# Attention with two sequences per tile: the weighted values of both in one full-width product per pair of heads

## What is computed

```python
attn = jax.nn.softmax(jnp.einsum('bhsd,bhtd->bhst', q, k) / sqrt(8), axis=-1)
out = jnp.einsum('bhst,bhtd->bhsd', attn, v)              # weighted values
out = out.transpose(0, 2, 1, 3).reshape(B, -1, D)
x = x + jnp.tanh(g_xattn) * (out @ Wo.T + bo)
```

## Time and profile before

| | before |
|---|---|
| median of 3 runs | 936.67 us (935.26 to 936.72) |
| the profiled execution's own time | 936.35 us |
| its span, first to last instruction | 934.5 us |
| busy share PE / DVE / ACT / POOL | 97% / 87% / 79% / 70% |
| TensorE's granted clock | 0.996 of full |

### The profile page before, as it was taken

The page is one execution under the profiler, slowest core; times in us unless marked ns, Lnnn a source line. Parts: engine busy times, 40 slices in busy tenths (PEclk is TensorE's granted clock), DMA queues, the critical chain, the costliest instruction groups (busy, mean ns, idle before and its releaser), DMA issues. The chain is left out here.

```text
span 934.5 us, 32489 instructions
## 1 busy us (share of the span) xinstructions
PE 906.0 (97%) x11654; PEld 736.1 (79%) x11654; DVE 811.1 (87%) x2348; ACT 742.8 (79%) x1617; POOL 652.9 (70%) x1184
## 2 busy tenths in 40 slices
PE   6999999999999999999899999999999999999996
PEld 3888788788889999998786777777777777777774
DVE  6898888899979998899778988898988868888886
ACT  5888888888887777776676788788878877888885
POOL 5787878776635566565989878778786638777773
PEclk9999999999999999999999999999999999999999
DMA  3501010100000000000000000000000003333333
GB/s 117 189 26 48 26 47 26 47 14 26 13 2 2 1 1 2 1 1 1 2 13 14 14 26 14 26 14 14 26 14 14 4 7 66 82 78 80 78 78 82
DMA packets 54270, 31.15 MB, mean 33 GB/s; under 512 B 38368, under 2 KB 46816, under 8 KB 54112
## 3 DMA queue, kind: packets, MB, share of 16 engines
q1 hardware_dynamic: 54112, 29.08, 11.7%
HBM read 16.48 MB, written 4.19 MB: 22 GB/s over the span
## 5 line engine op out<-in xcount | busy, mean ns | idle before, releaser
L1011 DVE TENSOR_REDUCE smax<-score 128x16 f32<-128x1024 f32 x128 | 156.6, 1224 | 44.7 <-PE score L1441 23.9
L1382 PEld LDWEIGHTS bank<-vb,prob_t 128*64 128x64 f32 x4096 | 130.2, 138 | 49.4 <-issue 40.9
L1023 DVE TENSOR_TENSOR prob<-score,smax 128x512 f32<-128x512 f32 x256 | 163.4, 680 | 0.4
L657 ACT ACTIVATE prob_t<-bank 128x512 f32<-128x512 f32 x256 | 139.1, 595 | 20.2 <-PE bank L1357 6.5
L652 ACT ACTIVATE prob<-prob 128x512 f32<-128x512 f32 x256 | 147.5, 632 | 5.4 <-DVE prob L1023 5.4
L1382 PE MATMUL bank<-vb,prob_t 128*64 128x18 f32 x4096 | 142.5, 212 | 0.1
L1357 PE MATMUL bank<-const,prob 128*128 128x128 f32 x1024 | 133.8, 274 | 0.7 <-DVE x_all L1124 0.7
L1357 PEld LDWEIGHTS bank<-const,prob 128*128 128x128 f32 x1024 | 116.4, 141 | 1.8 <-DVE x_all L1124 1.1
L736 ACT ACTIVATE eb_t<-eb,gwt 128x128 f32<-128x128 f32 x256 | 81.5, 390 | 40.0 <-POOL eb_acc L503 26.3
L663 ACT ACTIVATE o_t<-bank,b_col 128x128 f32<-128x128 f32 x128 | 48.8, 381 | 65.9 <-PE bank L1357 65.7
L435 POOL TENSOR_SCALAR kj<-k_sb,const 128x512 f32<-128x512 f32 x124 | 85.2, 694 | 20.7 <-issue 20.7
(11 more groups left out here) (171 smaller groups left out, 2335.3 us busy)
## 6 DMA issues: line engine op xcount, KB each, us to landing
ctx_t<-in_ctx SPq DMA_DIRECT2D x32, 256.0 KB, 2.7
x_all<-in_x SPq DMA_DIRECT2D x16, 256.0 KB, 3.4
out_x<-x_all SPq DMA_DIRECT2D x64, 64.0 KB, 1.8
ew<-in_ew SPq DMA_DIRECT2D x2, 512.0 KB, 6.0
q2t<-q2b SPq DMA_TRANSPOSE x64, 2.5
f_cw<-in_f_cw SPq DMA_DIRECT2D x1, 768.0 KB, 7.6
w_t<-in_w_attn SPq DMA_DIRECT2D x2, 256.0 KB, 4.2
f_w<-in_f_w SPq DMA_DIRECT2D x2, 256.0 KB, 7.0
```

Of the source, the lines that this page charges most:

```text
L657: act.activation(prob_t[:, 4 * half:4 * half + 4, :].rearrange("p i q -> p (i q)"), bank[(PT, PT2)[half]], ACT.Copy).then_inc(s["p_copied" ...
L1011: dve.tensor_reduce(smax[:].rearrange("p (r h) -> p r h", r=RH), sc, AX.X, ALU.max).then_inc(s["smax_done"], 1)
L1023: dve.tensor_tensor(prob[:, par, half * 512:(half + 1) * 512].rearrange("p (r h k) -> p r h k", r=2, k=S), sc[:, g], m.unsqueeze(3).to_bro ...
L1382: last = pe.matmul(bank[OV][q, i * 2 * VW:(i + 1) * 2 * VW], prob_t[:, i, q], vb[:, k // G, v0 + b * NPAIR + i, :, :].rearrange("p h v -> ...
```

## The change

The two products of a pair of heads become one. The stationary operand is all 128 columns of `prob_t` (both batches' queries), the streamed one the 18 columns of batch 0 and the 18 of batch 1, so the result is 128 x 2 x 18: each query row gets its weighted sum over the values of its own batch and one over those of the other batch, which is of no use. `divide` divides both (256 instead of 128 elements per partition); the denominator is the same for both. `transpose_o`, before a single transposition of 128 x 128, becomes two ordinary products with 64 columns of the identity each: the one for batch b has `o_n` of batch b as its stationary operand and streams the columns of the identity that pick the query rows of batch b.

The transposed outcome moves from the bank of the weighted values (`OV`) to the first columns of the bank `PT2`, which the second half of `transpose_p` also uses. `o_t` gets two buffers. In TensorE's program `transpose_o` now stands before `project_o`. Waits: the second half of `transpose_p(n)` now also waits for `o_copied` (`copy_o` of tile n-1); `transpose_o(n)` waits for `copy_o` of tile n-1 and for the copy of a second half from `PT2`; `values` no longer waits for `o_copied`; `divide` waits for `project_o` instead of `copy_o`.

```diff
-        o_tr_ps, wo_ps = bank[OV][:, 2 * P:3 * P], bank[OV][:, 3 * P:4 * P]
+        o_tr_ps, wo_ps = bank[PT2][:, 0:P], bank[OV][:, 3 * P:4 * P]
+        ov_ps = bank[OV][:, 0:BT * H * VW].rearrange("p (b c) -> p b c", b=BT)
...
-        o_n = sb("o_n", [P, 2, P])
-        o_t = sb("o_t", [P, P])
+        o_n = sb("o_n", [P, 2, BT, P])
+        o_t = sb("o_t", [P, 2, P])
...
             def divide(n, k):
-                ov = bank[OV][:, 0:H * VW].rearrange("p (h v) -> p h v", h=H)
+                ov = ov_ps.rearrange("p b (h v) -> p b h v", v=VW)
                 wait(dve, "pv_mm", n + 1)
-                wait(dve, "o_copied", n)
+                wait(dve, "wo_mm", n - 1)
...
-                dve.tensor_tensor(o_n[:, k % 2, :].rearrange("p (h v) -> p h v", h=H), ov[:, :, 0:HD],
-                                  rden[:].unsqueeze(2).to_broadcast([P, H, HD]), ALU.mult)\
+                dve.tensor_tensor(o_n[:, k % 2].rearrange("p b (h v) -> p b h v", v=HD), ov[:, :, :, 0:HD],
+                                  rden[:].unsqueeze(1).unsqueeze(3).to_broadcast([P, BT, H, HD]), ALU.mult)\
...
             def transpose_p(n, k, half):
                 wait(pe, "exp_done", 2 * n + half + 1)
                 wait(pe, "p_copied", 2 * n + half - 1)
+                if half:
+                    wait(pe, "o_copied", n - 1)
...
-                wait(pe, "o_copied", n - 1)
                 for i in range(NPAIR):
...
-                    for b in range(BT):
-                        q = slice(b * S, (b + 1) * S)
-                        last = pe.matmul(bank[OV][q, i * 2 * VW:(i + 1) * 2 * VW], prob_t[:, i, q],
-                                         vb[:, k // G, v0 + b * NPAIR + i, :, :].rearrange("p h v -> p (h v)"),
-                                         start=True, stop=True, skip_group_check=True)
+                    last = pe.matmul(ov_ps[:, :, i * 2 * VW:(i + 1) * 2 * VW], prob_t[:, i, :],
+                                     vb[:, k // G, v0 + i:v0 + BT * NPAIR:NPAIR, :, :].rearrange("p b h v -> p b (h v)"),
+                                     start=True, stop=True, skip_group_check=True)
...
             def transpose_o(n, k):
                 wait(pe, "o_norm", n + 1)
-                tr(o_tr_ps, o_n[:, k % 2, :]).then_inc(s["o_tr"], 1)
+                wait(pe, "o_copied", n)
+                wait(pe, "p_copied", min(2 * n + 4, 2 * T * (n // T + 1)))
+                for b in range(BT):
+                    q = slice(b * S, (b + 1) * S)
+                    last = pe.matmul(o_tr_ps[:, q], o_n[:, k % 2, b, :], ident[:, q], start=True, stop=True)
+                last.then_inc(s["o_tr"], 1)
```

More of the change, by code:

```diff
@@ L661, in copy_o @@
                 wait(act, "o_tr", n + 1)
-                wait(act, "wo_mm", n)
-                act.activation(o_t[:].rearrange("p (s b) -> p b s", b=BT),
+                wait(act, "wo_mm", n - 1)
+                act.activation(o_t[:, n % 2, :].rearrange("p (s b) -> p b s", b=BT),
                                o_tr_ps.rearrange("p (b s) -> p b s", b=BT),
@@ L973, in masks, with residual @@
                 dve.tensor_scalar(neg_mask[:], m_keep[:], 1.0, NEG, ALU.subtract, ALU.mult).then_inc(s["mask_v"], 1)
-            def residual(n, t, read=None):
+            def residual(n, t):
                 wait(dve, "wo_mm", n + 1)
-                wait(dve, "o_copied", n + 2 if read is None else read)
                 wait(dve, "bo_added", n + 1)
@@ L981, in divide @@
             def divide(n, k):
-                ov = bank[OV][:, 0:H * VW].rearrange("p (h v) -> p h v", h=H)
+                ov = ov_ps.rearrange("p b (h v) -> p b h v", v=VW)
                 wait(dve, "pv_mm", n + 1)
-                wait(dve, "o_copied", n)
+                wait(dve, "wo_mm", n - 1)
                 wait(dve, "o_norm", n)
-                dve.reciprocal(rden[:], ov[:, :, HD]).then_inc(s["rden_done"], 1)
+                dve.reciprocal(rden[:], ov[:, 0, :, HD]).then_inc(s["rden_done"], 1)
                 wait(dve, "rden_done", n + 1)
-                dve.tensor_tensor(o_n[:, k % 2, :].rearrange("p (h v) -> p h v", h=H), ov[:, :, 0:HD],
-                                  rden[:].unsqueeze(2).to_broadcast([P, H, HD]), ALU.mult)\
+                dve.tensor_tensor(o_n[:, k % 2].rearrange("p b (h v) -> p b h v", v=HD), ov[:, :, :, 0:HD],
+                                  rden[:].unsqueeze(1).unsqueeze(3).to_broadcast([P, BT, H, HD]), ALU.mult)\
                     .then_inc(s["o_norm"], 1)
@@ L1239, in attention0_tail @@
                 group_stats(3, 1)
-                residual(n, n, n + 1)
+                residual(n, n)
                 relu(0, 0, 7)
@@ L1343, in attention1_tail @@
                 lead_in(ffn, 1, 1)
-                residual(n, t, n + 1)
+                residual(n, t)
             dve.wait_ge(s["sc_set"], 2)
@@ L1393, in project_o @@
                 wait(pe, "x_attn", n)
-                pe.matmul(wo_ps, o_t[:], w_t[:, L, 3, :], start=True, stop=True)\
+                pe.matmul(wo_ps, o_t[:, n % 2, :], w_t[:, L, 3, :], start=True, stop=True)\
                     .then_inc(s["wo_mm"], 1)
@@ L1445, in step @@
                         values(n - 2, (k - 2) % 8)
+                    if has(-3):
+                        transpose_o(n - 3, (k - 3) % 8)
                     if has(-4):
                         project_o(L, n - 4)
-                    if has(-3):
-                        transpose_o(n - 3, (k - 3) % 8)
                     if has(-1):
@@ L1622, in attention0_tail @@
                 values(n - 1, (n - 1) % 8)
+                transpose_o(n - 2, n - 2)
                 project_o(0, n - 3)
-                transpose_o(n - 2, n - 2)
                 transpose_p(n, n % 8, 0)
```

## The result

The changed kernel takes 1075.1 us (median of 4, 1073.67 to 1076.48) against 936.69: a ratio of 1.148, 95% interval 1.1463 to 1.1497. Slower was forecast, at 1090 us and between 1062 and 1117; the time moved by 138.4 us where 153 were forecast. The profiled execution took 1074.79 us.

What follows compares the result with a forecast made beforehand. TensorE was taken to bound the attention, VectorE close behind. 128 tiles x 1.07 = 137 us, plus 19 us of stand-still, less 3 us at the ends, made +153 us on 936.35: 1090 us, range 1062 to 1117.

Steps and rivals of the forecast that it cites:

- stand-still: TensorE waiting for `copy_o` at `transpose_p`'s second half: 0.15 us a tile, 19 us over some 124 tiles.
- the rival without a stand-still: `copy_o` is back in time, so TensorE does not wait at `transpose_p`: 1070 us, or 1062; chance 15%.
- The bound and the price of a pass: TensorE bounds the attention; a pair of 64-column loads costs 58 ns, one 128-column load 111 ns.
- the per-tile term of 1.07 us: TensorE from `values` to `project_o`: 22 full-width passes at 111 ns, 2.45 us against 1.38 before.
- the gap of 0.12: TensorE's idle time behind the narrow `values`, where the array goes from halves to whole; 0.12 us a tile, taken as gone.
- TensorE's own way to that place: From `transpose_o` to `transpose_p`'s second half: two passes of `project_o` and four of the first half, 0.66 us.
- The ends: New TensorE work fitting into its waits at the ends of both layers' attention: 3 us taken back, 0 to 7.
- `divide`: VectorE's division of 256 instead of 128 elements: 0.12 us more a tile, hidden in VectorE's waits.
- Passes priced by the piece: In `values`, a wide load costs no more than a narrow one, 29 ns: about 908 us; chance 3%.
- Load and stream one after the other: Wide loads cannot run beside the stream before, so 20 new passes also pay theirs: at most 280 us more; chance 2%.

Runs made afterwards that it cites:

- experiment 1: Changed kernel with `values` again as 16 narrow 64-column products, each streaming the 36 columns of both batches: 983.14 us.
- experiment 6: Changed kernel with `divide` writing each batch's useful 64 partitions in its own VectorE operation, and `transpose_o` again a single transposition: 1034.07 us.
- experiment 3: Kernel before with `transpose_o` as two ordinary products of 64 identity columns each instead of one transposition: 970.75 us.
- experiment 7: Changed kernel with the transposed outcome in the bank of `transpose_p`'s first half, so that the first half waits for `copy_o`: 1164.8 us.
- experiment 4: Changed kernel's order, banks, buffers and waits, but narrow 18-column products, `divide` on 128 elements and one transposition as before: 944.23 us.
- experiment 9: Changed kernel's wide products with `divide` picking the useful half, one transposition, and `prob_t` and `vb` in bfloat16: 940.62 us.
- experiment 2: Changed kernel with each of the 8 wide products streaming only batch 0's 18 columns, batch 1's weighted values left out: 1137.11 us.

## Why the prediction was right, and which term was off

The mechanism held, and the range too; the number was 15 us too long. That brings the result near to another branch: the forecast rests on a stand-still of 0.1 to 0.2 us a tile (1076 to 1103 us), and the measured 1075.1 us lies just below that, between it and the rival without a stand-still (1062 to 1070 us).

**The bound and the price of a pass** stood as put. The 22 passes from `values` to `project_o` take 2.45 us as priced from the earlier trace rows, so the per-tile term of 1.07 us is what the trace after shows. The rows before with the streams of 2 and 68 columns, which the price rests on, and the new one with 36:

```profile
250.46 0.28 PE L1597 MATMUL bank<-f_s,const 128*128 128x2 f32 x2
...
250.60 1.09 PE L1541 MATMUL bank<-gate_w,mxt 128*128 128x68 f32 x8
```

```profile
155.07 1.98 PE L1381 MATMUL bank<-vb,prob_t 128*128 128x36 f32 x16
```

Experiments 1 and 6 find 0.72 and 0.70 us of it in the width of `values` alone (forecast: 0.85 less the gap of 0.12, 0.73), experiments 3 and 6 find 0.27 and 0.32 us in `transpose_o` (0.33 forecast).

**The stand-still was mis-sized**: 0.15 us a tile was taken, 0.04 measured, 19 us against 5, which is nearly all of the 15 us. The rows after:

```profile
157.24 0.28 PE L1392 MATMUL bank<-const,o_n 128*128 128x64 f32 x1
...
157.55 0.39 ACT L664 ACTIVATE o_t<-bank,b_col 128x128 f32<-128x128 f32 x1 [1.42 <-PE bank L1392]
```

```profile
158.05 0.20 PEld L1357 LDWEIGHTS bank<-const,prob 128*128 128x128 f32 x2
```

ScalarE's side came out as priced: `copy_o` starts 0.31 us after the last matmul of `transpose_o`, takes 0.39, and the fifth load of `prob` follows 0.11 us after its end (so in all 124 steps that have both), 0.81 us in all against 0.80. The term that failed is TensorE's own way to that place, put at 0.66 us. That counts the six passes in between; but the fifth product of `prob` is the seventh pass, so its matmul is due 7 x 0.11 = 0.77 us after the last one of `transpose_o`, which leaves 0.03 to 0.04. In the rows the fifth load, due 0.11 us after the fourth at 157.96, starts at 158.05, 0.09 late; but the loads run some 0.11 us ahead of their matmuls (157.52 and 157.63 for the first of `prob`), so that only about 0.04 reaches the step. Moved ahead by four transpositions (experiment 7) the same wait costs 0.43 us; with a single transposition in front (experiments 4 and 6) 0.09.

**The ends** were taken at 3 us given back. 128 x (1.07 + 0.04) = 142 us against 138.4 leaves 4; by the traces it is about 5, since the stretches outside the steps also grew, by 3.3 us. From the first load of `values` to that of the last step, layer 0 takes 240.4 us before and 307.9 after, layer 1 257.9 and 325.6: 135.2 us more, where 126 steps of 1.11 would be 140. Part of it is to be seen in the last steps of layer 1, where TensorE waited for VectorE before the change and no longer does; the start of the mask products before and three steps later, then the same after:

```profile
739.12 0.40 PE L1433 MATMUL score<-neg_mask,ident 64*128 64x256 bf16 x4 [0.36 <-DVE prob L1023]
...
750.96 0.39 PE L1433 MATMUL score<-neg_mask,ident 64*128 64x256 bf16 x4 [0.36 <-DVE prob L1023]
```

```profile
873.24 0.39 PE L1437 MATMUL score<-neg_mask,ident 64*128 64x256 bf16 x4
...
886.85 0.39 PE L1437 MATMUL score<-neg_mask,ident 64*128 64x256 bf16 x4
```

Three steps went from 11.84 to 13.61 us: 0.59 us more each instead of 1.11. The rest of the 5 us I did not follow up.

**`divide`** costs VectorE 0.13 us (0.42 instead of 0.29; 0.12 was forecast) and nothing in time: over 1 us a tile of VectorE's idle time covers it.

**The rivals.** Passes priced by the piece: refuted by the 111 ns of L1381, in float32. In bfloat16 a wide load cost no more than a narrow pair (experiment 9). Load and stream one after the other: refuted by experiments 1 and 2, in which the stream's length (18 or 36 columns) leaves the loads' spacing as it is.

## What to carry to other kernels

Where a small float32 product reloads its stationary operand each time, count passes by the width of their load, not products: two 64-column loads side by side cost 58 ns (with 18, 36 or 64 streamed columns), one of 128 columns 111 ns (with 2 to 128), so merging a pair into one full-width product nearly doubles TensorE's time for it even though it halves the instructions. With far more columns behind a load the stream counts again: the products of K (L1408 to L1410, 512 columns) start 0.23 us apart in the changed kernel (158.79 and 159.02). Before merging, look for a row of the same width and type in the trace, since in bfloat16 the width was free here; and ask which engine handles the half that is thrown away. A wait that a shared bank brings is cheap only as long as other work lies between it and what it waits for: the same wait four transpositions earlier cost ten times as much, 0.43 us instead of 0.04. And when two engines race to one point, count the passes up to and with the one that waits: one pass too few made 0.04 us into 0.15.

## What was not expected of the hardware

Less streaming made TensorE slower. With 18 instead of 36 columns behind each wide load, TensorE as busy as before, the granted clock fell to 1.2 GHz in parts of the attention (mean 0.82 of 2.4 GHz from 620 to 900 us), 62 us in all; with 36 columns it stayed at 1.00. With a stand-still of half a microsecond a step it fell too, to 0.91 and 0.98 on average, some 36 us. Narrow loads in pairs with 18 columns, in the kernel before, kept the full clock. And putting a single transposition ahead of a two-pass product, directly behind the narrow pairs, saved 0.06 us in the step shown and 3 us in all, as its load and the next one start together.
